# One-off weight work at a decoder kernel's start: low parts made in halves, and a norm set ahead of the lambda and value parts

## The reference

```
x = x + attn(layernorm(x), Wq, Wk, Wv, Wo, lq1, lk1, lq2, lk2)

def attn(x, ...):                       # 16 heads of 2 halves of 16 channels
    q, k, v = x @ Wq * scaling, x @ Wk, x @ Wv
    aw = softmax(q k^T + causal)        # 32 maps
    lam = exp(sum(lq1 * lk1)) - exp(sum(lq2 * lk2)) + LAMBDA_INIT
    aw = aw[first halves] - lam * aw[second halves]
    attn = rmsnorm(aw @ v) * (1 - LAMBDA_INIT)
    return attn @ Wo
```

## Time and profile before

| | |
|---|---|
| time, median of 3 runs | 4060.63 us (4058.48 to 4062.3) |
| profiled execution, its own time | 4065.1 us |
| its span | 4063.3 us |
| granted TensorE clock, mean over the span | 0.985 |
| busy over the span | PE 96%, PEld 76%, DVE 71%, ACT 58%, POOL 43% |
| chain that ended last | PE 84%, DMA 5%, DVE 4%, ACT 3%, issue 2% |

### The profile page before, as it was taken

How to read it: one execution, slowest core, us unless ns; L and a number is a source line. 1 busy time by engine, 2 the same in 40 slices (tenths; PEclk the granted TensorE clock), 3 DMA queues, 4 the chain that set the end, 5 groups by cost and what they waited for, 6 DMA issues and landing times.

```text
span 4063.3 us, 74219 instructions
## 1 busy us (share of the span) xinstructions
PE 3904.8 (96%) x24605; PEld 3091.9 (76%) x24698; DVE 2877.9 (71%) x6053; ACT 2355.4 (58%) x5466; POOL 1759.6 (43%) x2191
## 2 busy tenths in 40 slices
PE   6999999979999999999899999999999999999999
PEld 6888888744444444444589999999999999999998
DVE  5677766657888888888557777777777777777333
ACT  4777777637777777777535555555555555555111
POOL 1222332233555555555325555555555555554210
PEclk9999999969999999999999999999999999999999
DMA  5000000023333333344148888888888888887421
GB/s 194 17 27 22 22 22 22 19 81 106 116 117 117 114 113 117 117 137 138 39 134 244 255 252 253 250 257 255 249 253 249 252 253 253 253 250 215 151 89 60
DMA packets 289801, 618.53 MB, mean 152 GB/s; under 512 B 71648, under 2 KB 80224, under 8 KB 289424
## 3 DMA queue, kind: packets, MB, share of 16 engines
q1 hardware_dynamic: 221136, 453.83, 34.1%
q0 software_dynamic: 67136, 157.86, 16.0%
q10 hardware_dynamic: 1152, 2.10, 0.1%
HBM read 461.81 MB, written 151.26 MB: 151 GB/s over the span
## 4 chain that ended last, share of the span: by engine, by line
PE 84%; DMA 5%; DVE 4%; ACT 3%; issue 2%; SPq 1%; POOL 0%; ACTq 0%; POOLq 0%; DVEq 0%
PE ps L515 19%; PE ps L517 17%; PE ps L516 17%; PE ps L687 6%; PE ps L502 4%; PE ps L648 3%; PE ps L537 3%; PE ps L670 3%; DMA XI<-x_normed,TI 3%; PE ps L786 3%; PE ps L610 2%; PE ps L812 2%; ACT PX L962 2%; PE ps L531 1%; DMA DL<-in_w_down 1%
## 5 line engine op out<-in xcount | busy, mean ns | idle before, releaser
L515 PE MATMUL ps<-WG,XT 128*128 128x352 f32 x2416 | 801.9, 332 | 7.3 <-DVE XT L1466 4.8
L516 PE MATMUL ps<-WG,XT 128*128 128x352 f32 x2416 | 779.8, 323 | 0.0
L517 PE MATMUL ps<-WG,XT 128*128 128x352 f32 x2416 | 779.8, 323 | 0.0
L962 ACT ACTIVATE PX<-ps 128x1024 f32<-128x1024 f32 x512 | 523.3, 1022 | 259.8 <-PE ps L670 252.7
L1289 DVE TENSOR_REDUCE NM<-ps 128x2 f32<-128x1024 f32 x512 | 622.4, 1218 | 71.5 <-PE ps L648 67.3
L1769 POOL DMA_INDIRECT sum<-YO,TI x238 | 394.0, 1655 | 643.7 <-issue 552.0
L1472 DVE TENSOR_TENSOR HS<-ps,HS 128x352 f32<-128x352 f32 x302 | 158.4, 524 | 544.9 <-ACT HS L1104 543.3
L1104 ACT ACTIVATE HS<-ps 128x352 f32<-128x352 f32 x302 | 140.7, 466 | 585.0 <-PE ps L517 585.0
L515 PEld LDWEIGHTS ps<-WG,XT 128*128 128x128 f32 x2416 | 455.1, 188 | 7.7 <-DVE XT L1466 4.9
L1430 DVE TENSOR_TENSOR WG<-WL,WG 128x704 fp32r<-128x704 f32 x524 | 448.7, 882 | 15.0 <-ACT WG L1074 14.9
L516 PEld LDWEIGHTS ps<-WG,XT 128*128 128x128 f32 x2416 | 455.5, 189 | 0.0
(11 more groups left out here) (267 smaller groups left out, 8805.0 us busy)
## 6 DMA issues: line engine op xcount, KB each, us to landing
WL<-in_w_gate SPq DMA_DIRECT2D x127, 704.0 KB
WL<-in_w_up SPq DMA_DIRECT2D x127, 704.0 KB
DL<-in_w_down SPq DMA_DIRECT2D x127, 512.0 KB
kq_parts<-HL SPq DMA_DIRECT2D x64, 512.0 KB, 3.0
KS<-kq_parts SPq DMA_DIRECT2D x384, 64.0 KB
QS<-kq_parts SPq DMA_DIRECT2D x384, 64.0 KB
DL<-in_w_down SPq DMA_DIRECT2D x127, 192.0 KB
CB<-sum POOLq DMA_DIRECT2D x64, 256.0 KB, 3.0
```

Source lines behind the costliest of these rows:

```text
L515: pe.matmul(out_, lh(0), rh(0), start=first, stop=False)
L516: pe.matmul(out_, lh(0), rh(1), start=False, stop=False)
L517: return pe.matmul(out_, lh(1), rh(0), start=False, stop=last)
L962: act.activation(PX[:, n % 4, :, :], ps[:, 5 * 512:7 * 512], ACT.Exp, scale=0.25).then_inc(S["a_px"], 1)
```

## The change

The two one-off operations on WA become four on each engine: by halves of the columns, and in each half the queries' weights before the keys'. q(0) and k(0) wait for the pieces of columns 0 to 255, q(1) and k(1) for those of columns 256 to 511. On VectorE, `begin_a` is taken from behind `evict_k(0)` and stands behind `norm_x(2)`, the next step of VectorE's in the order. On ScalarE `begin_a` stays behind `evict_q(0)`. All later counts on the two semaphores go up by two.

```
             def q(n):
                 pe.wait_ge(S["l_xl"], 2 * (n // 2) + 2)
-                if n == 0:
-                    pe.wait_ge(S["v_ws"], 1)
+                if n < 2:
+                    pe.wait_ge(S["v_ws"], 2 * n + 1)
...
             def k(n):
-                if n == 0:
-                    pe.wait_ge(S["v_ws"], 2)
-                elif n < 5:
+                if n < 2:
+                    pe.wait_ge(S["v_ws"], 2 * n + 2)
+                if 0 < n < 5:
                     pe.wait_ge(S["v_kT"], n)
-                else:
+                if n >= 5:
                     pe.wait_ge(S["v_x1"], n - 4)
                 project(6, 1, n).then_inc(S["p_k"], 1)
...

...
             def begin_qk():
 
                 act.wait_ge(S["d_qk"], 32)
-                for w in range(2):
-                    act.activation(WAH[:, w, :, :], WA[:, w, :, :], ACT.Copy).then_inc(S["a_ws"], 1)
+                for h in range(2):
+                    for w in range(2):
+                        act.activation(WAH[:, w, :, 256 * h:256 * h + 256], WA[:, w, :, 256 * h:256 * h + 256],
+                                       ACT.Copy).then_inc(S["a_ws"], 1)
...
             def low_b(w):
-                dve.wait_ge(S["a_ws"], w + 3)
+                dve.wait_ge(S["a_ws"], w + 5)
...
             def begin_qk():
 
-                for w in range(2):
-                    dve.wait_ge(S["a_ws"], w + 1)
-                    dve.tensor_tensor(WAL[:, w, :, :], WA[:, w, :, :], WAH[:, w, :, :].bitcast(f32),
-                                      ALU.subtract).then_inc(S["v_ws"], 1)
+                for h in range(2):
+                    for w in range(2):
+                        at = slice(256 * h, 256 * h + 256)
+                        dve.wait_ge(S["a_ws"], 2 * h + w + 1)
+                        dve.tensor_tensor(WAL[:, w, :, at], WA[:, w, :, at], WAH[:, w, :, at].bitcast(f32),
+                                          ALU.subtract).then_inc(S["v_ws"], 1)
...
                     if name == "norm_x" and n == 1:
                         begin_qk()
-                    if name == "evict_k" and n == 0:
+                    if name == "norm_x" and n == 2:
                         begin_a()
```

More of the change, by code:

```diff
@@ L587, in v @@
                     e.then_inc(S["p_bo"], 1)
-                    pe.wait_ge(S["v_ws"], 3)
+                    pe.wait_ge(S["v_ws"], 5)
                 for c in range(4):
@@ L626, in wo @@
                 if b == 0:
-                    pe.wait_ge(S["v_ws"], 4)
+                    pe.wait_ge(S["v_ws"], 6)
                 for c in range(4):
@@ L701, in rotate @@
                 if b == 0:
-                    pe.wait_ge(S["v_ws"], 7)
+                    pe.wait_ge(S["v_ws"], 9)
                 bank0("v_t", 4 * b + 2 * kq + pm + 1)
@@ L1254, in begin_qk @@
             def begin_qk():
-                for w in range(2):
-                    dve.wait_ge(S["a_ws"], w + 1)
-                    dve.tensor_tensor(WAL[:, w, :, :], WA[:, w, :, :], WAH[:, w, :, :].bitcast(f32),
-                                      ALU.subtract).then_inc(S["v_ws"], 1)
+                for h in range(2):
[4 more added lines that the diff above has]
+                                          ALU.subtract).then_inc(S["v_ws"], 1)
             def split_w():
                 for k, (low, raw, high) in enumerate(((WXL, WX, WXH), (WVL, WV, WVH), (WOL, WO, WOH))):
-                    dve.wait_ge(S["a_ws"], k + 5)
+                    dve.wait_ge(S["a_ws"], k + 7)
                     dve.tensor_tensor(low[:], raw[:], high[:].bitcast(f32), ALU.subtract).then_inc(S["v_ws"], 1)
```

## The result

The changed kernel takes 4053.7 us in the median of 21 runs (4048.13 to 4058.9), the kernel before 4061.2 us in 21 runs beside it (4056.93 to 4065.89). The ratio is 0.9981, 95% interval 0.9974 to 0.9988: faster by 4.9 to 10.6 us. The forecast was 4052.8, a gain of 7.86. The profiled execution has a span of 4057.0 us at a mean grant of 0.984, against 4063.3 at 0.985.

The account below looks back on a forecast made before the run. TensorE was taken as the bound, busy 3904.8 of 4063.3 us, so start-up savings carry to the end. 1.54 + 4.68 + 1.92 - 0.28 = 7.86 us gave a median of 4052.8, range 4048.5 to 4057.

Parts of the forecast that it names:

- Part 1: Weights by halves ahead of q(0): first product at 19.83 instead of 21.37, gain 1.54 us, bounds 1.16 to 1.91.
- meeting with GpSimd: VectorE's first WAL piece waits until GpSimd's XTS subtraction ends at 18.44; without it the sum would be 0.37 us larger.
- Part 2: Third batch's norm on VectorE ahead of the lambda and value work, right behind evict_k(0): gain 4.68 us.
- cover: Slack of 0.45 us before v(0) on TensorE waits for q(1)'s delayed evictions; beyond it delay shows one for one.
- Part 3: q(1) and k(1) on TensorE at 2.4 GHz after a gap of about 1.2 us: gain 1.92 us, lower bound 0.
- Part 4: Fourth batch's norm waits for GpSimd's copy, held by VectorE's WBL subtraction: loss 0.28 us, bounds 0 to 0.9.
- finish line: Fourth batch's transposes on TensorE, at 47.48 us before, forecast near 39.6; behind them neither engine's order is changed.
- Rival D: Gain swallowed by a later wait on a transfer not moved: 0 to 3 us left, 4057.6 to 4060.6; chance 0.05.
- rival B: Clock falls in the new 1.2 us gap or rises later under q(0): price 1.9, sum 5.9, 4054.7 us; chance 0.12.
- Rival C: Low clock stretches further on fall otherwise: gain 11.3 (4049.4) or 4.5 us (4056.2); chance 0.19.
- rival E: Slower: shifted start tips the remaining 42 us of the 775 to 900 us passage to low clock, 34 net (4095); chance 0.02.
- sign of being wrong: Distance between the two traces of 8 us at 50 us and another one at 775 or 900.

Follow-up runs that it names:

- weights_ahead: Changed kernel with ScalarE making the weight pieces of columns 0 to 255 ahead of copy_x(1), the other two behind low_xt(1); ratio to the kernel before 0.9982.
- changed_again: The changed kernel run once more beside later follow-ups, nothing altered; ratio to the kernel before 0.9983, median 4057.18 us.
- wv_low_later: Changed kernel with begin_o (second half of the WBL subtraction) put behind norm_x(3) instead of in front of it; ratio to the kernel before 0.9991.
- move_only: Kernel before with only begin_a moved behind norm_x(2), weights not halved; ratio to the kernel before 0.9976.
- cover_gone: Changed kernel with two added 1024-element reductions ending begin_a on VectorE; third to fourth batch's transposes 13.23 us, against 10.05 in the changed kernel.
- warm_gap: Kernel before with 36 unread products put behind k(0) on TensorE, nothing moved; ratio to the kernel before 0.9997.
- no_copy: Changed kernel without GpSimd's copy of the mean in the first stage's norms; third to fourth batch's transposes 9.82 us, 0.23 less.
- late_start: Changed kernel with 12 unread 1024-element reductions on VectorE ahead of the first stage; ratio to the kernel before 1.0016.

## Why the prediction was right, step by step

**Part 1, the halves**, forecast 1.54. From the first xn to the first product it is 11.20 us instead of 12.90: 1.70. The meeting with GpSimd is real but was priced too high. WAL's first piece is not seen to wait until GpSimd was through; it began at 17.89 and took 1.446 instead of 1.21, so the meeting cost 0.24, not 0.37. weights_ahead, whose first two pieces meet nothing, has them in 2.36 us together, and in 2.58 the other two, which meet the same GpSimd operation.

The Trainium skill, page "SBUF — State Buffer", section "Who interferes with whom", calls the port that the two engines share an exclusive lock: who issues first has it, the other blocks in full. In this trace both directions are seen, VectorE's first piece lengthened by 0.24 us and GpSimd's one-element copy by 1.64. The second agrees with the page; for the first the measured 0.24 is less than the 0.36 for which GpSimd was still busy.

**What the sum left out.** From the first product to evict_k(0) it is 7.65 us instead of 8.28, 0.63 more of gain. Products are 0.21 us apart at first and 0.12 from 23.3 us on, 3.8 us after the first; before, it was 5.2 us after the first. In changed_again, the same kernel, the distance from first product to evict_k(0) is 8.13, in wv_low_later 8.64, in move_only 8.70. So this term has both signs from one execution to the next, and it belongs to the scatter, not to the change.

**Part 2, the move**, forecast 4.68. From evict_k(0) to xn it is 0.61 instead of 5.29: 4.68. The cover was 0.45 by the forecast; ScalarE's qA ends at 34.35 and evict_k(1) begins at 34.68, so it is 0.3. cover_gone shows that the cover is needed, and that beyond it the price was more than one for one in that execution.

**Part 3, the clock**, forecast 1.92. From the 3rd transposes to evict_k(1) it is 6.35 instead of 8.48: 2.13. The grant was 1.00, and the transposes overlap the first product more than I took. warm_gap, which has the same 6.35 with nothing moved, shows that this is the clock's doing.

**Part 4, what is late next**, forecast -0.28. From evict_k(1) to xn of the fourth batch it is 3.10 instead of 2.87: -0.23, and no_copy gives exactly 0.23 back. The sum of the four parts measured is 1.70 + 4.68 + 2.13 - 0.23 = 8.28; with 0.63 from the clock under q(0) it is 8.91, and with the constants' 0.19 the 9.10 of the finish line.

**From there to the end.** Rival D, a swallowed start with 0 to 3 us left, is out by the median (at least 4.9) and by the distance of 8.6 us that is left at 775 us; late_start agrees. Of rival B, the clock did not fall in the new gap in any of the executions with that gap; its other half, a rise that comes later under q(0), did come about in move_only and wv_low_later. Rivals C and E are about the clock further on, and there the median's distance of 7.5 instead of 8.3 to 8.9 may lie; it is inside the interval. Rival C describes what the profiled pair did: the low stretch at 71 to 78 us is gone, others at 61 and 88 have come. In rival E the stretch at the full level is 32% of 125, 40 us and not 42, which changes nothing.

**What was luck.** The prediction named a sign of being wrong: a distance between the traces that is 8 us at 50 us and another one at 775 or 900. At 775 it was 8.6 against 9.1, but at 905 it was 12.1, and 6.3 at the end. The prediction's step from 50 us to the end, that the work behind runs as before, holds for the waits (the distance stays at 8.6 us from 300 to 775 us) and not for the clock of a single execution. The steps of the first 50 us are shown by the traces; that the medians' distance came out within 0.4 us of the sum, with an interval of 2.9 us to each side, is in part luck. How much the clock matters can be seen in the runs of the changed kernel: the fastest, 4048.13, had a mean grant of 0.988, and the slowest, 4058.9, one of 0.985. The scatter goes with the grant, and it is larger than the whole effect. Why a stretch is low in one execution and not in the next these runs do not settle.

## What to carry to other kernels

In a kernel that is bound by one engine, as this one is, a microsecond taken off ahead of its first dense stretch is about one at the end; look there for one-off work that stands in an in-order queue ahead of something the bound engine waits for, and move it behind. Price the gap twice: once for its length, and once for the low clock behind it, here 4.7 us less of gap, and 2.1 for the clock. Trust the second price less: in warm_gap it was given back within a few microseconds by a fall of the clock elsewhere. Changes of 0.2% are told by times in the trace before and after, with the clock's share taken out, and only in the sum by the median. When large two-operand work on VectorE is moved, look what GpSimd does meanwhile: a one-element copy can then take 1.8 us.

## What was unexpected of the hardware

A wait of 2.0 us on TensorE cost more than itself (cover_gone): the clock fell only after v(0) had begun again to work. And the length of the wait does not tell alone. The wait of 1.24 us ahead of the third batch's transposes had no such effect in any execution; the one of 1.51 us ahead of q(2), the same in all kernels here, had none in ten of the twelve traces, while in warm_gap and wv_low_later the grant behind it was 0.50 for some 3 us. Why there, these runs do not settle.

GpSimd's copy was held for 1.64 us by a VectorE subtraction, while its power operation, 0.57 us long and begun 0.13 before that subtraction, was not lengthened at all. The copy of 1.82 us behind a power operation of 0.57 is in move_only and changed_again as well. In these traces it was the operation begun second that took longer.
